# Swin blocks and iterative whitening in one core: when denominators are packed, where the next block's weight preparation runs, and how pair transposes are split

## The reference

```
for shift, mask in ((0, MASK0), (3, MASK1)):
    y = layer_norm(x, ln1); y = roll(y, -shift)
    wins = y in 7x7 windows                    # 256 windows of 49 tokens, 64 channels
    q, k, v = wins @ qkv_w + qkv_b             # 8 heads of 8 channels
    attn = softmax(q k^T / sqrt(8) + rel_bias + mask)
    out = (attn @ v) @ proj_w + proj_b; out = roll back
    x = x + out
    x = x + gelu(layer_norm(x, ln2) @ fc1 + b1) @ fc2 + b2
# whitening: groups of 16 channels, covariance over all tokens, 5 Newton steps for cov^(-1/2)
out = gamma * (W (x - mean)) + beta
```

## Time and profile before

| | us |
|---|---|
| three runs | 744.16, 745.93, 752.17 |
| median | 745.93 |
| the profiled execution | 749.74 |
| its span, first to last instruction | 747.9 |
| mean granted TensorE clock | 0.972 of full |

### The profile page before, as it was taken

One profiled execution on the slowest core, in us unless ns is written; L12 is line 12 of the kernel. 1 busy time (PEld: TensorE's weight loads), 2 busy tenths in 40 slices (PEclk: granted clock), 3 DMA queues, 4 the chain that ended last, 5 costly groups with the idle time before them and its releaser, 6 DMA issues.

```text
span 747.9 us, 27067 instructions
## 1 busy us (share of the span) xinstructions
PE 682.8 (91%) x11578; PEld 407.5 (54%) x11578; DVE 518.4 (69%) x910; ACT 363.2 (49%) x629; POOL 215.1 (29%) x505
## 2 busy tenths in 40 slices
PE   5889889999999999899799999999999969999787
PEld 3456556656666654344355566656665544335567
DVE  3867886888688575899657887788887545881233
ACT  2365454455545456576255455545554564764200
POOL 5001212124122112476401123223211214996000
PEclk9999999999999999999889999999999999999759
DMA  7411111122112111000011122112111210000014
GB/s 194 101 43 57 53 50 49 49 72 65 55 50 76 60 34 48 1 1 1 28 41 49 55 69 68 50 55 79 57 49 57 64 39 12 2 1 1 2 34 139
DMA packets 47628, 37.57 MB, mean 50 GB/s; under 512 B 28564, under 2 KB 47124, under 8 KB 47508
## 3 DMA queue, kind: packets, MB, share of 16 engines
q1 hardware_dynamic: 41744, 33.09, 14.6%
q10 hardware_dynamic: 5764, 2.74, 1.4%
HBM read 18.15 MB, written 4.01 MB: 30 GB/s over the span
## 4 chain that ended last, share of the span: by engine, by line
PE 64%; DVE 11%; ACT 10%; issue 9%; SPq 2%; ACTq 2%; DMA 1%; POOL 0%; DVEq 0%; POOLq 0%
PE psum L1083 62%; ACT pt L546 6%; ACT vbd L537 2%; ACTq L557 2%; ACT osb L553 1%; DVE nmax L846 1%; DVE lt L829 1%; PE psum L1531 1%; DVE lt L830 1%; SPq L285 1%; DVE ly L831 1%; DMA XW<-x_dram 1%; DVE ly L827 1%; DVE XW L980 1%; PE psum L1305 1%
## 5 line engine op out<-in xcount | busy, mean ns | idle before, releaser
L846 DVE TENSOR_REDUCE nmax<-psum 113x16 f32<-113x784 f32 x128 | 118.8, 970 | 97.8 <-PE psum L1083 97.8
L436 POOL TENSOR_TENSOR att<-osb,rec 128x392 f32<-128x392 f32 x64 | 74.1, 1160 | 372.5 <-DMA rec<-dens 372.1
L546 ACT ACTIVATE pt<-psum 113x784 f32<-113x784 f32 x128 | 98.6, 824 | 91.3 <-PE psum L1083 91.3
L1083 PE MATMUL psum<-bt,rows_r 117*113 117x392 f32 x256 | 77.0, 405 | 3.5 <-DVE nmax L846 1.2
L1083 PE MATMUL psum<-pt,vbd 113*32 113x49 f32 x4096 | 59.5, 209 | 4.0 <-ACT osb L553 3.9
L1083 PE MATMUL psum<-kexp,qsb 32*49 32x196 f32 x2048 | 59.3, 338 | 1.0 <-DMA kexp<-ksb 1.0
L505 ACT ACTIVATE lv<-psum,epsc 128x392 f32<-128x392 f32 x30 | 17.6, 588 | 87.4 <-PE psum L1083 87.4
L1083 PEld LDWEIGHTS psum<-pt,vbd 113*32 113x32 f32 x4096 | 50.6, 110 | 15.7 <-issue 14.5
L1083 PE MATMUL psum<-qexp,ksb 32*49 32x196 f32 x2048 | 58.7, 336 | 0.0
L396 POOL TENSOR_TENSOR XW<-XW,wcol 128x49 f32<-128x49 f32 (+5 forms) x200 | 55.5, 316 | 9.5 <-DVE XW L980 9.3
L1083 PE MATMUL psum<-att,wph 128*64 128x196 f32 x512 | 49.5, 334 | 8.9 <-ACT vbd L537 5.5
(11 more groups left out here) (186 smaller groups left out, 1174.6 us busy)
## 6 DMA issues: line engine op xcount, KB each, us to landing
rec<-dens SPq DMA_DIRECT2D x64, 196.0 KB
kexp<-ksb SPq DMA_DIRECT2D x128, 49.0 KB
qexp<-qsb SPq DMA_DIRECT2D x128, 49.0 KB, 2.3
XW<-x_dram SPq DMA_DIRECT2D x14, 196.0 KB, 4.3
out_dram<-XW SPq DMA_DIRECT2D x14, 196.0 KB, 2.4
dpk<-osb ACTq DMA_DIRECT2D x64, 12.2 KB
dens<-rpk SPq DMA_DIRECT2D x64, 12.2 KB, 1.8
conb<-c_all_dram ACTq DMA_DIRECT2D x1, 760.0 KB, 7.2
```

The costliest lines, as they stand in the source:

```text
L436: nc.gpsimd.tensor_tensor(att[:, 4 * part:4 * part + 4, :], osb[part][:, :].rearrange("p (a n) -> p a n", a=4), rec[part][:, :].rearrange( ...
L546: nc.scalar.activation(pt[grp][:, b:b + 2, :], SC[0:KROWS, b:b + 2, 0:BANK], ACT.Exp)\
L846: nc.vector.tensor_reduce(nmax[:, b:b + 2, grp, :], SC[0:KROWS, b:b + 2, 0:BANK].rearrange("p a (k m) -> p a k m", m=NTOK), AX.X, ALU.max, ...
L1083: return nc.tensor.matmul(o, a, b, start=start, stop=stop, **k)
```

## The change

Three things are moved; the amount of computation is the same.

- `o_copy` is split: the copy stays, the packing DMA becomes `pack`. In a step, `pack(G-1, 1)` is issued behind `evac_v`, not in front of it. `pack(G, 0)` stays behind `o_copy(G, 0)`.
- The DVE part of block 1's preparation piece runs inside `anorm`, behind the sixth chained instruction, instead of after the step.
- `to_channels` and `window_order` can do one part alone. Pairs i = 5, 6, 7 move to steps 1, 2, 3 (before: 0, 1, 2), part 0 in the old place, part 1 behind the projection (on ACT behind `square`). `TBANK` changes: the second part of i = 1 goes into `bX`, and i = 5, 6, 7 all go into `bO`. K of step 0 waits only for i = 4.

```diff
-        TBANK = [PS[1], PS[2]] + [bA] * 4 + [bA, bO] * 3 + [bO] * 4
+        TBANK = [PS[1], PS[2], bA, bX, bA, bA] + [bA, bO] * 2 + [bO] * 6
...
-            def window_order(i):
+            def window_order(i, *parts):
...
-                for part, (t0, tn) in enumerate(WGROUPS):
+                for part in parts or range(2):
+                    t0, tn = WGROUPS[part]
...
                 nc.scalar.activation(osb[part][:, :], bO[:, 0:4 * NROWS], ACT.Copy).then_inc(osb_done, 1)
+
+            def pack(g, part, first=False):
+
                 act.wait_ge(osb_done, 2 * g + part + 1)
...
                 if ahead > 0:
                     evac_v(G + 1, 1 - u, f)
+                if not first:
+                    pack(G - 1, 1, base == 0 and g == 1)
                 if f:
                     window_order(3)
                     window_order(4)
-                elif base == 0 and g < 3:
-                    window_order(5 + g)
+                elif base == 0 and g < 4:
+                    window_order(4 + g, 0)
...
                     square(G + 3)
+                if base == 0 and 0 < g < 4:
+                    window_order(4 + g, 1)
+                if ahead > 2:
                     variance(G + 3, 1 - u)
-                if f:
-                    window_order(5)
...
                 o_copy(G, 0, f)
+                pack(G, 0, f)
...
-                    anorm(G + 3, 1 - u, {4: lambda: spread_max(G + 1)})
+                    anorm(G + 3, 1 - u, {4: lambda: spread_max(G + 1), 6: piece or (lambda: None)})
...
-                    step(p, blk, base, g, g % 2, min(3, HALVES - 1 - g))
-                    if blk == 0:
-                        block_one(g)
+                    step(p, blk, base, g, g % 2, min(3, HALVES - 1 - g),
+                         piece=(lambda: block_one(g)) if blk == 0 else None)
...
-                elif blk == 0 and g < 3:
+                elif blk == 0 and g < 4:
                     pe.wait_ge(osb_done, 2 * G)
-                    to_channels(5 + g)
+                    to_channels(4 + g, 0)
...
                     proj(p, G - 2)
+                if blk == 0 and 0 < g < 4:
+                    to_channels(4 + g, 1)
...
-                if first and blk == 0:
-                    to_channels(5)
...
-                            pe.wait_ge(s_tpcp, 12)
+                            pe.wait_ge(s_tpcp, 10)
...
-                if blk == 0 and 0 < g < 3:
-                    pe.wait_ge(s_tpcp, 2 * (6 + g))
+                if blk == 0 and 0 < g < 4:
+                    pe.wait_ge(s_tpcp, 2 * (5 + g))
```

More of the change, by code:

```diff
@@ L672, in _ @@
                 o_copy(base + HALVES - 1, 1)
+                pack(base + HALVES - 1, 1)
                 nxt = base + HALVES
@@ L877, in residual, with step @@
                                                ALU.add, ALU.add).then_inc(res_done, 1)
-            def step(p, blk, base, g, u, ahead, last=None):
+            def step(p, blk, base, g, u, ahead, last=None, piece=None):
                 G = base + g
@@ L1263, in start @@
                 pe.wait_ge(k_done, base + 1)
+                if blk == 0:
+                    pe.wait_ge(z_done, 1)
                 if blk:
@@ L1283, in start @@
                 else:
+                    pe.wait_ge(s_tpcp, 4)
                     f_xc(0, 2)
@@ L1292, in start, with to_channels @@
                     f_q(p, base + 1, bO)
-            def to_channels(i):
+            def to_channels(i, *parts):
                 b = XORDER[i]
```

## The result

| | before | after |
|---|---|---|
| median of 6 runs, us | 746.25 | 735.4 |
| lowest to highest | 744.16 to 752.17 | 732.88 to 739.26 |
| profiled execution | 749.74 | 739.26 |
| its span | 747.9 | 737.4 |

The ratio is 0.9847, 95% interval 0.9804 to 0.989: 10.9 us faster. The forecast was 14.3 less (731.6), so the time is in the range and 3.8 us above the predicted one. Two later comparisons of the same two kernels gave 0.9846 and 0.9812.

What follows compares the result with a forecast made beforehand. TensorE's own sequence and its waits bound the kernel (64% of the span). Packing 6.3, pieces 4.8 and transposes 3.2 sum to 14.3 off the median 745.9, giving 731.6 us; range 727 to 740.

Steps and rivals of the forecast that it cites:

- The packing: Denominators' DMA issue moved behind V's evictions: PE's projection no longer waits, 0.30 us per plain step, 6.3 us in all.
- the packed denominators come 1.25 us later: Steady steps: issuing behind V's evictions delays the denominators 1.25 us, still 0.4 us before DVE's second reciprocal, costing nothing.
- The limit of 2.64: Reciprocal hidden up to 2.2 us of copy time, DVE's rest to 2.64; beyond, each 0.1 costs 0.1 in 28 steps.
- rival 1: Denominators too late: DVE's second reciprocal, residual, row maxima and PE's scores are delayed, kernel ends slower; chance 0.05.
- The pieces: Block 1's preparation inside the norm: PE's V matmuls in four early steps stop waiting for DVE, saving 4.8 us.
- port rule: DVE and GpSimd share one port pair, the second is blocked; stalled weight scalings would make z 0.35 us later.
- Rival 3: First steps: the norm's z misses PE, part of the 4.8 returns; with half the transposes lost too, 735.6; chance 0.15.
- The transposes: Pair transposes in two parts, steps 0 to 3: 2.2 + 0.55 + 1.2 - 0.7 = 3.2 us saved.
- the first scores wait for K's spread by DMA there: Prologue: the new bank removes a wait of at most 1.3 us, but this wait covers it, so counted as zero.
- Rival 2: Steady gain returns as ACT waiting for GpSimd's product before copying P·V; all 6.3 lost gives 738; chance 0.12.

Runs made afterwards that it cites:

- pack_square: Changed kernel with the packing DMA issue put still later, behind `square`, in all steps that have one: 734.27 us, 0.9809 of before.
- pack_sq_done: Changed kernel with the packing issue behind `square` and waiting until `square` has ended: 734.2 us, 0.9796 of before.
- split_old: Kernel before with only the transposes split in two parts, keeping the prologue's old bank for pair 1: 745.69 us, 0.9962 of before.
- after_again: The changed kernel run again, unaltered, for a second profile: 736.97 us, 0.9846 of before, span 732.1.
- old_prologue: Changed kernel with the second part of pair 1 back in its old bank in the prologue: 733.54 us, 0.9795 of before.
- after_third: The changed kernel run once more, unaltered, in the third batch: 735.8 us, 0.9812 of before.
- best: Changed kernel with the prologue's old bank, and six late input loads and block 1's bias loads behind the second half's spreads: 733.29 us, 0.9783 of before.

## Why the prediction was right, and where not

**The packing: right in size, wrong in one step.** 6.3 forecast, 6.6 measured alone, and 0.30 per plain step in the profile (14.87 to 14.57). The projection at 0.56, no wait for `vbd`, and no idle DVE before the reciprocals came as said. The step "the packed denominators come 1.25 us later" failed: they come no later at all. The rows show the issue running beside the evictions, so the 0.60 that stood in front of V's evictions is hidden beside them. The order decides only whether they wait for the issue. The error was harmless, since `pack_square` and `pack_sq_done`, which do bring the denominators later, lost nothing.

**The limit of 2.64 (rival 1) was wrong too.** It counted DVE's idle time before the second row maxima as the last reserve. Issued 2.3 us later than in after, with DVE waiting in 24 more places than in after, the kernel is as fast (0.9796). PE's own K and Q projections lie between, and this reserve wasn't counted. What held PE up first, in the one step that went too far, was not on the forecast's list as a wait of PE: the residual, which K's projection waits for. By that step the limit is about 5.8 us behind V's matmuls, 0.6 later than the forecast's.

**The pieces: right.** 4.8 forecast, 4.5 measured alone. z came later by the piece and was covered, by 0.36 where 0.6 was worked out, or 0.25 with the scalings held up by GpSimd. The port rule of the Trainium skill (SBUF — State Buffer, Who interferes with whom) agrees again with the trace, that DVE's L838 (L829 before) takes 1.26 us where its neighbours take 0.57, while GpSimd multiplies beside it. Rival 3 did not come true: the sum of steps 1 to 5 leaves no room for a late z.

**The transposes: the term that was mis-sized.** 3.2 forecast; alone, 0.9 lost (1.0012) with the new bank and 2.8 gained (0.9962) with the old one, in two different batches. Its steps in the profile are near what was said: step 0 shortens by 2.1 (2.2 forecast) where the clock stays up, and the wait between the parts in step 1 went from 1.26 to 0.80 (0.71 by the forecast), and that in step 2 is gone. What the sum leaves out is the wait of step 0's scores for the spread of half 1's K. The prediction costs the prologue at zero because "the first scores wait for K's spread by DMA there", and for half 0 that held: the weight load of its first scores waited 0.47 and waits 1.43 and 1.60 in the two profiles of after. But PE then also reaches the scores of half 1 sooner, and their K is issued on SP no sooner (39.31 against 39.25). This second wait has no price in the prediction. It was 0.52 in before's profile and 0 to 3.2 us over all 14, and behind each long one came some 9 us at the lower clock; together they make a step 0 of 23.6 instead of 17.6 us. It occurs with the old bank too (`split_old`), so it is not shown to come from the change. The spans with and without it, 10.5 (after) and 15.8 (`after_again`) under that of before, stand on either side of 14.3, though 1.9 of both is the stretch behind the last V matmuls, which varies by itself. That this episode is where the missing 3 us of the medians went is argued from the profiles, not shown: it would need its frequency in the runs that have no profile.

**Rival 2 is half there.** ACT's wait for `att` went from 3.9 to 7.4 us, as it said, but the steps kept their 0.30. With the packing alone it went to 5.0 in 6 places, and the whole 6.3 came. That ACT's idle time behind that copy covers the wait, as the forecast held against it, fits this, but no run isolates it.

**Left open.** How much is missing, and why. The three comparisons of the changed kernel gave 10.9, 11.5 and 14.1 us (0.9847, 0.9846, 0.9812); their mean ratio, 0.9835, is 12.3 us of 746.25. The parts alone with the new bank sum to 6.6 + 4.5 - 0.9 = 10.2, with the old bank to 6.6 + 4.5 + 2.8 = 13.9, near the forecast. That would point to the new bank as what costs some 3 us, but it sets the first batch against the third. Inside a batch the two banks lie about 1 us apart: `pack_square` 0.9809 and `old_prologue` 0.9795 in the second, `after_third` 0.9812 and `best` 0.9783 (which has the loads moved too) in the third, with intervals of 0.3 to 0.4% on each. No profile shows a cost of the bank itself. So no cost of the new bank is shown. `best` at 733.29 is the fastest measured, by less than the intervals.

## What to carry to other kernels

Before costing a moved DMA issue on ScalarE, look in the trace whether the issue starts at the end or at the start of the activations in front of it; behind them it was free here, in front of them its 0.60 us held PE up by 0.30 us in each plain step. A wait of an early matmul for a DMA isn't a fixed number from one profile: read it in several executions, and price its long form with the lower clock behind it. A limit on lateness is counted along every result that stands behind the late one, up to the first instruction of the bounding engine that needs one of them, with the work that this engine has before it: here that was the residual in front of K's projection, and not the row maxima. And a gain ahead of a DMA whose issue comes no sooner is lost to the wait for it.

## What the runs showed of the hardware

- A DMA issue queued behind two activations of 0.59 us started 0.15 us after the first one's start and 0.46 before the second one's, and one behind a 0.50 us `square` 0.06 after its start: ACT issues beside running activations.
- Where PE idled 2.90, 3.14 and 3.19 us in step 0, the granted clock fell to 0.50 (1.2 GHz) within the wait and stayed there for some 9 us behind it, though PE was busy for 8.8 of the 10 us from 44 to 54 in after; score matmuls took 1.59 instead of 0.91 us. With idle times up to 1.1 us at the same place they took 0.91.
- A slow matmul is not always seen in the rows of the granted clock. In the prologue the same 32 score matmuls (half 0) took 1.29 to 1.59 us in 8 of the 14 profiles, and in three of them, before's among them (1.58 at 28.08), the row gives 1.00 there.
- The small copy from `osb` to `dpk` took 1.81 us from the start of its issue to the waiting reciprocal, as in the earlier trace rows (1.82), and 2.46 once.
